# Each score matmul of 128 keys issued as four matmuls of 32 keys

## The reference

```
k = layernorm_per_head(x @ Wk.T) * scale        # 16 heads x 16 dims, scale = 256 ** -0.25
q = layernorm_per_head(x @ Wq.T) * scale
v = x @ Wv.T
dot = einsum('bihd,bjhd->bhij', q, k);  dot = where(causal, -inf, dot)
att = softmax(dot);  out = einsum('bhij,bjhd->bihd', att, v) @ Wo.T + bo
```

## Time and profile before

| | us |
|---|---|
| median of three executions | 1194.99 |
| lowest, highest | 1192.07, 1195.09 |
| span of the profiled execution, first to last instruction | 1192.3 |
| PE matmuls busy | 1104.1 (93%), 8884 records |
| ACT busy | 1014.7 (85%) |
| DVE busy | 467.5 (39%) |
| POOL busy | 241.6 (20%) |

### The profile page before, as it was taken

The page is one execution under the profiler, slowest core; times in us unless marked ns, Lnnn a source line. Parts: engine busy times, 40 slices in busy tenths (PEclk is TensorE's granted clock), DMA queues, the critical chain, the costliest instruction groups (busy, mean ns, idle before and its releaser), DMA issues.

```text
span 1192.3 us, 22761 instructions
## 1 busy us (share of the span) xinstructions
PE 1104.1 (93%) x8884; PEld 359.6 (30%) x8884; DVE 467.5 (39%) x1181; ACT 1014.7 (85%) x1134; POOL 241.6 (20%) x377
## 2 busy tenths in 40 slices
PE   3758999999999999999999999999999999999994
PEld 3534333332323233232332232232222222222123
DVE  5678665554544353333333323423131222021114
ACT  3216788789888998999999999999999999999980
POOL 2236533222122211212022021012110101010100
PEclk9779999999999999999999999999999999999996
DMA  5022202003000300003000022000001100000000
GB/s 145 3 63 60 59 11 81 1 28 99 1 1 19 93 17 1 1 32 92 4 1 1 1 67 60 1 1 2 1 10 48 53 1 1 10 10 1 1 19 18
DMA packets 39608, 33.37 MB, mean 28 GB/s; under 512 B 8722, under 2 KB 39432, under 8 KB 39496
## 3 DMA queue, kind: packets, MB, share of 16 engines
q1 hardware_dynamic: 37364, 31.74, 9.0%
q10 hardware_dynamic: 2132, 0.12, 0.1%
HBM read 18.73 MB, written 12.85 MB: 26 GB/s over the span
## 4 chain that ended last, share of the span: by engine, by line
PE 72%; ACT 13%; issue 6%; DVE 6%; DMA 1%; POOL 1%; SPq 0%; ACTq 0%; DVEq 0%; POOLq 0%
PE ps L1190 68%; ACT ring L776 13%; PE ps L1232 2%; PE ps L1298 1%; DMA x<-in_x 1%; DVE st L807 1%; PE ps L1252 1%; DVE area L828 1%; DVE oT L1159 0%; POOL rstd L711 0%; POOL sq L532 0%; DVE x L980 0%; DVE ss L985 0%; DVE sq L1013 0%; ACT area L765 0%
## 5 line engine op out<-in xcount | busy, mean ns | idle before, releaser
L776 ACT ACTIVATE ring<-ps 128x1024 f32<-128x1024 f32 x1056 | 982.2, 1115 | 65.5 <-PE ps L1190 63.5
L1190 PE MATMUL ps<-ring,vf 128*17 128x512 f32 (+3 forms) x4608 | 559.4, 562 | 5.0 <-DVE oT L1159 4.4
L1190 PE MATMUL ps<-queries,keys 50*128 50x512 f16 (+3 forms) x2304 | 363.2, 366 | 22.1 <-ACT ring L776 4.9
L1190 PEld LDWEIGHTS ps<-queries,keys 50*128 50x128 f16 x2304 | 92.3, 93 | 475.3 <-ACT ring L776 437.3
L724 POOL TENSOR_SCALAR_AFFINE_SELECT ring<-ring 128x256 f32<-128x256 f32 (+1 forms) x224 | 103.9, 481 | 396.5 <-ACT ring L776 392.6
L1190 PEld LDWEIGHTS ps<-ring,vf 128*17 128x17 f32 x4608 | 79.7, 95 | 174.5 <-issue 144.2
L711 POOL TENSOR_TENSOR rstd<-var,minus_half 128x4 f32<-128x4 f32 x24 | 24.4, 1017 | 235.6 <-DVE var L813 235.4
L980 DVE SCALAR_TENSOR_TENSOR x<-ps,power,x 128x512 f32<-128x512 f32 x32 | 24.0, 750 | 110.7 <-PE ps L1190 110.7
L846 DVE CAST xnT<-ps 128x512 f16<-128x512 f32 x32 | 22.1, 691 | 100.0 <-PE ps L1232 100.0
L1190 PE MATMUL ps<-baseT,xnT 128*128 128x256 f16 x384 | 55.0, 283 | 3.9 <-DVE area L848 3.8
L1232 PE MATMUL ps<-ident,area 128*128 128x128 f32 x192 | 34.2, 311 | 20.0 <-DVE area L828 20.0
(11 more groups left out here) (153 smaller groups left out, 670.5 us busy)
## 6 DMA issues: line engine op xcount, KB each, us to landing
parts_d<-split SPq DMA_DIRECT2D x32, 256.0 KB, 2.6
keys<-parts_d SPq DMA_DIRECT2D x96, 64.0 KB, 2.3
queries<-parts_d SPq DMA_DIRECT2D x192, 32.0 KB
x<-in_x SPq DMA_DIRECT2D x8, 512.0 KB, 4.2
out_x<-x SPq DMA_DIRECT2D x16, 256.0 KB, 2.2
queries<-shift_d SPq DMA_DIRECT2D x64, 4.0 KB
ring<-in_base_W SPq DMA_DIRECT2D x1, 256.0 KB, 4.9
ring<-in_Wq SPq DMA_DIRECT2D x1, 256.0 KB, 3.8
```

The lines of the kernel that those rows point to most:

```text
L776: act.activation(probs[:, u % RING, :], bank(2 * (u % SLOTS), 2), ACTF.Exp, bias=0.0, scale=1.0).then_inc(exp_ok, 1)
L1190: return pe.matmul(o, lhsT, rhs, start=start, stop=stop, skip_group_check=True)
```

## The change

Every score matmul is issued as four, each with 32 of the 128 keys as its stationary operand and all the queries as its moving one, writing 32 PSUM partitions. The matmuls of the two heads (row halves) alternate within each column group. A unit of full width has thus eight matmuls of 50 rows x 32 columns x 512 queries instead of two of 50 x 128 x 512. The semaphore is still raised by the last one alone. Nothing else is touched.

```diff
-                for h, j, q0, w, b, col in blocks:
-                    half = slice(HR * (h % 2), HR * (h % 2) + SH + 2)
-                    m = mm(bank(2 * (u % SLOTS) + b)[:, col:col + w], keys[half, h // 2, j * P:(j + 1) * P],
-                           queries[half, h // 2, q0:q0 + w], True, True)
+                for first, second in zip(blocks[0::2], blocks[1::2]):
+                    for k in range(0, P, 32):
+                        for h, j, q0, w, b, col in (first, second):
+                            half = slice(HR * (h % 2), HR * (h % 2) + SH + 2)
+                            m = mm(bank(2 * (u % SLOTS) + b)[k:k + 32, col:col + w], keys[half, h // 2, j * P + k:j * P + k + 32],
+                                   queries[half, h // 2, q0:q0 + w], True, True)
                 m.then_inc(s_ok, 1)
```

## The result

| | before | changed |
|---|---|---|
| median of five executions, us | 1195.09 | 1202.91 |
| lowest, highest | 1192.07, 1196.54 | 1200.13, 1204.40 |
| ratio to before, 95% interval | | 1.0071 [1.0052, 1.0089] |
| span of the profiled execution | 1192.3 | 1202.0 |

The changed kernel is slower by 0.71%, 8.5 us by the ratio. Beside the later experiments it was timed once more, at 1.0065 [1.0039, 1.0091]. The forecast was 1206, slower.

What follows compares the result with a forecast made beforehand. PE was taken to bound three quarters of the attention and share the end with ACT. Of 592 score runs, 452 on the chain x 24 ns = 10.8, taken as 11 us: 1195.0 + 11 = 1206 us, range 1199 to 1211.

Steps and rivals of the forecast that it cites:

- part 1: Score matmuls on PE: queries streamed once per column group, all side by side, 0 us; if halves in turn, 248 us.
- part 2: End of each unbroken run of score pairs: six more tile starts, 24 ns, over 592 runs 14.2 us of PE time.
- part 3: Start of a score run: 9216 weight loads of 32 columns cost nothing extra; bounds 43 and 98 ns if loaded in turn.
- part 4: PE's switches between scores and other work: the 0.10 us gap stays since rows still differ, 0 us.
- part 5: PE's instruction supply: 13824 more instructions, 0.9 MB on queues at 0.5% together, taken as 0 us.
- From PE time to span: Added PE time lengthens the span only where PE is on the chain: 10.8 us of 14.2, taken as 11 us.
- rival C: The added delay vanishes in PE's short waits for ACT: no change that can be told, 1195 us; chance 0.15.
- Rival A: Score-values switches no longer wait: 83 us of PE time go before 900 us, perhaps 45 won, 1150 us; chance 0.12.
- Rival D: All eight score loads in turn, or slower sustained matmul issue: 452 x 0.095 = 43 us, 1238 us; chance 0.07.
- the eight starts: Profile's score rows: eight matmuls of a pair at 0.41 us instead of two at 0.39.
- the 0.34 us to the next kind: PE's timeline: from a score run's start to the next kind of work, 0.34 us instead of 0.32.
- the unmoved 0.98 us behind the values: PE's timeline: from a values batch's start to the following scores, 0.98 us as before.

Runs made afterwards that it cites:

- 64-column kernel: Against the kernel before, each score matmul issued as two of 64 keys (64 x 64 tiles), where the change has four of 32; measured ratio 1.0050 [1.0032, 1.0068].

## Why the prediction was right

It named the direction, and 1206 is 3 us from the measured 1202.9. That it is so near is in good part luck. Step by step:

- **Streaming** (part 1), 0 us: right. Row halves and column groups run at once.
- **The starts** (part 2), 24 ns a run: 20 ns measured. The score pair was the right row to take: 16 instructions start within 23 ns, so the 3.1 ns for an instruction that was read from the values' loads, and the 39 ns from it, do not hold for these tiles. With 592 runs the array time was 10.5 us where the sum had 14.2.
- **The loads** (part 3), 0: right in the number, for 32 columns (89 ns a load). The bounds rested on loads in turn; what the 64-column kernel points to is another cost, the length of an unpacked load, 13 ns a run. The Trainium skill (TensorEngine Tiling, Restrictions and Gotchas) says that column tiling excludes the fast weight load, and the trace agrees with it: 64 columns take 104 ns where 128 took 93.
- **The switches** (part 4), 0: right, and shown by the kernel in which both kinds agree and the 0.10 us goes.
- **The instructions** (part 5), 0: wrong. They are about half of the loss, 4.5 us with the array time taken away. The step looked at the rate of PE and at the load of the queues, 0.5%, and not at who else is held up while a packet comes, which is SP.
- **From PE time to span**, 76%: wrong. 30% of a like amount shows, 44% of a large one. The step took the chain's lengthening as a floor; the runs show that it isn't one. PE's waits for ACT between two score pairs, 53 us before, take up what is added in front of them: 33 us of 58, 7.6 of 10.6. The 0.43 us that was read for such a wait is the idle time of the weight loads; by the starts, 1036.34 and 1036.87, PE's own wait is 0.30. That such waits swallow added time is the mechanism of rival C, which had 0.15.

So the sum came near by two errors that cancelled: 11 us by a share twice too large, where the runs give about 4 us of array time and 4 us with the instructions. Without the second part the kernel would have come to about 1199, at the lower edge of the range. Rival A was priced far too high as well: 50 us of array time less brought 11 us, 22%, so 83 us less would have brought some 18 and not 45 (an estimate by that share). Rival D's price was worked out with 95 ns where part 3 has 98, which makes 1239 of 1238. Of the signs, the eight starts, the 0.34 us to the next kind, the unmoved 0.98 us behind the values and ACT's waits, 8.5 us longer before 900 us and not behind, all came as said.

## What to carry to other kernels

Cutting a matmul into column groups gained nothing here, since its tiles still differed in rows from their neighbours', and it added 20 ns to each of 592 runs; the gap went only where rows and columns both agreed. Where two engines are both nearly full, read how much the second waits on the first and the other way round before turning one engine's time into span; a pair of knobs that add and take away a known amount gives the share in two runs (here 44% and 22%). Many more instructions on one engine can slow another that only issues transfers: compare the packets of the instruction queue and the longest issues. And side work that seems to cost a switch may be standing in a wait.

## What the runs showed of the hardware

Tiles of 50 rows and 32 columns, eight at a time, start 3.3 ns apart in either order and stream together. The next matmul in the same kind of tile needs no gap; between kinds of tiles there is one of 0.10 us, whether rows or columns differ. A load of 64 float16 columns took 104 ns on average, of 32 columns 89, of 128 packed ones 93. A fourfold number of score matmuls cost 4.5 us [3.0, 6.2] with no array time added, which nothing in the busy rows would have told. While a 16 KB packet of instructions came in, an issue of a transfer on SP could take 0.9 to 2.0 us instead of 0.28 to 0.45; no issue after 100 us was that long without one, and their number went from 8 to 16 as the packets went from 73 to 127.
